# Moving the split of the projection weights from GpSimd to ScalarE and VectorE, a block of fills later in SyncE's queue, and the expert splits into another order

## The reference

```python
q = (layernorm(x) @ Wq)            # 16 heads of 64
k, v = (y @ Wkv)
res = softmax(q @ k.T * 64 ** -0.5) @ v
x = x + res @ Wproj + bproj
p = softmax(layernorm(x) @ gate_w); top 2 of 8, shares normalised
hidden = silu(h @ gate_w_e) * (h @ up_w_e)      # 512 wide
x = x + sum over the two of share * (hidden @ down_w_e)
```

## Time and profile before

| | |
|---|---|
| median of 3 runs | 1500.26 us (1498.55 to 1500.38) |
| the profiled execution | 1500.38 us |
| its span | 1498.6 us |
| PE busy | 1461.8 us (98%) |
| DVE, ACT, POOL busy | 950.6, 732.1, 550.7 us |
| mean granted TensorE clock | 0.994 |

### The profile page before, as it was taken

One profiled execution on the slowest core, in us unless ns is written; L12 is line 12 of the kernel. 1 busy time (PEld: TensorE's weight loads), 2 busy tenths in 40 slices (PEclk: granted clock), 3 DMA queues, 4 the chain that ended last, 5 costly groups with the idle time before them and its releaser, 6 DMA issues.

```text
span 1498.6 us, 37285 instructions
## 1 busy us (share of the span) xinstructions
PE 1461.8 (98%) x11882; PEld 1289.0 (86%) x11883; DVE 950.6 (63%) x2600; ACT 732.1 (49%) x2032; POOL 550.7 (37%) x641
## 2 busy tenths in 40 slices
PE   6999999999999999999999999999997999999997
PEld 5888889888888988898889888888886888888886
DVE  5667777677767776767777777767668543333332
ACT  4555555555555555555555555555556322222221
POOL 3424334343434343433334343434354332233222
PEclk9999999999999999999999999999998999999999
DMA  9222222222222222222222222213027233333332
GB/s 253 86 66 68 74 73 72 68 73 66 72 72 72 75 92 80 76 72 66 72 73 72 69 72 66 76 40 108 29 80 260 56 59 54 51 49 50 52 53 25
DMA packets 101105, 113.80 MB, mean 76 GB/s; under 512 B 17244, under 2 KB 88140, under 8 KB 101068
## 3 DMA queue, kind: packets, MB, share of 16 engines
q1 hardware_dynamic: 87900, 94.33, 20.6%
q0 software_dynamic: 12144, 15.66, 6.4%
q10 hardware_dynamic: 1024, 3.34, 0.7%
HBM read 61.37 MB, written 51.93 MB: 76 GB/s over the span
## 4 chain that ended last, share of the span: by engine, by line
PE 94%; DVE 3%; DMA 1%; issue 1%; ACT 0%; POOLq 0%; DVEq 0%; SPq 0%
PE bank L1375 25%; PE bank L1318 17%; PE bank L1444 11%; PE bank L1420 10%; PE bank L1410 9%; PE bank L1638 7%; PE bank L1465 6%; PE bank L1382 4%; PE bank L1622 2%; PE bank L1577 1%; DVE probT L1187 1%; DVE Wgu L1056 1%; PE bank L1492 1%; DMA WqL_whole<-in_L_xattn_Wq 1%; PE bank L1482 0%
## 5 line engine op out<-in xcount | busy, mean ns | idle before, releaser
L844 ACT ACTIVATE prob<-bank,neg_max 112x375 f32<-112x375 f32 x512 | 298.7, 588 | 135.7 <-DVE neg_max L1181 135.7
L1181 DVE TENSOR_REDUCE neg_max<-bank 112x1 f32<-112x375 f32 x512 | 243.7, 538 | 16.0 <-PE bank L1410 15.9
L1420 PE MATMUL bank<-ident,prob 112*125 112x112 f32 x1536 | 214.5, 273 | 2.7 <-ACT prob L844 2.4
L1420 PEld LDWEIGHTS bank<-ident,prob 112*125 112x125 f32 x1536 | 195.9, 188 | 13.8 <-ACT prob L844 4.8
L779 POOL DMA_INDIRECT out<-y_out,dest_now x63 | 98.1, 1557 | 221.6 <-ACT y_out L931 196.5
L1444 PE MATMUL bank<-probT,V 125*64 125x112 f32 x3072 | 176.5, 264 | 1.9 <-DVE probT L1187 1.1
L1318 PE MATMUL bank<-Wgu,hT_h 128*128 x504 | 177.1, 433 | 1.0 <-DVE hT_l L1247 1.0
L1444 PEld LDWEIGHTS bank<-probT,V 125*64 125x64 f32 x3072 | 149.0, 137 | 28.4 <-issue 25.1
L969 DVE TENSOR_TENSOR K_l<-bank,K_h 128x376 fp32r<-128x376 f32 x256 | 140.2, 549 | 51.6 <-ACT K_h L804 45.3
L959 DVE COPY V<-bank 125x512 f32<-125x512 f32 x96 | 66.4, 692 | 137.7 <-PE bank L1382 134.7
L802 ACT COPY V<-bank 125x512 f32<-125x512 f32 x96 | 56.3, 587 | 181.3 <-PE bank L1382 178.7
(11 more groups left out here) (196 smaller groups left out, 3587.8 us busy)
## 6 DMA issues: line engine op xcount, KB each, us to landing
bins<-pad_rows SPq DMA_DIRECT2D x29, 1032.0 KB, 5.8
inv_rows<-sums SPq DMA_DIRECT2D x126, 128.0 KB, 2.8
h_in<-bins SPq DMA_DIRECT2D x63, 129.0 KB, 2.1
Wgu<-in_L_ffn_gate_up_w SPq DMA_DIRECT2D x6, 1024.0 KB, 7.8
y_sb<-in_ctx SPq DMA_DIRECT2D x32, 187.5 KB, 2.6
y_sb<-in_ctx SPq DMA_DIRECT2D x62, 93.8 KB, 2.6
x_sb<-in_x SPq DMA_DIRECT2D x16, 224.0 KB, 2.9
x_res<-in_x SPq DMA_DIRECT2D x32, 112.0 KB, 2.4
```

Of the source, the lines that this page charges most:

```text
L844: nc.scalar.activation(prob[:, j, :], S_ps[j][0:LQ, 0:LKV], ACT.Exp, bias=neg_max[:, j:j + 1], accum_out=row_sum[:, head // HB, head % HB: ...
L1181: nc.vector.tensor_reduce(neg_max[:, j:j + 1], S_ps[j][0:LQ, 0:LKV], AX.X, ALU.max, negate=True).then_inc(max_done, 1)
L1420: last = nc.tensor.transpose(S_ps[j][0:KR, t * LQ:t * LQ + LQ], prob[:, j, t * KR:t * KR + KR], ident[0:LQ, 0:LQ])
```

## The change

Three things are changed.

1. SyncE: the wait for the split of b = 1 and the load of y of b = 3 stand ahead of the bins' fills instead of behind them.
2. The projection weights: GpSimd's `split_projection` (four copies and four subtractions on quarters, behind `split_O` of b = 0) is gone. ScalarE copies all of `WpH` in one instruction at the end of b = 0, s = 1, and VectorE subtracts all of `WpL` in one at the end of b = 0, s = 3.
3. The handover to the experts: ScalarE copies expert 4 before it issues the loads of experts 6 and 7, and expert 6 behind the rows of tiles 0 and 1 instead of ahead of them. VectorE subtracts experts 4 and 5 behind the rows instead of ahead of them.

```diff
             load_y(2, 0)
             sp.wait_ge(xn_done, 2)
             load_x(1)
+            sp.wait_ge(y_lo, 2)
+            sp.wait_ge(yB_lo, 2)
+            sp.wait_ge(yT_done, 2)
+            load_y(3, 1)
             sp.wait_ge(pads_ready, 1)
             sp.dma_start(bins[E * STRIDE:E * STRIDE + IDLE * P, :].rearrange("(n p) w -> p n w", p=P),
                          pad_rows[:].unsqueeze(1).to_broadcast([P, IDLE, W])).then_inc(idle_out, 16)
             for k in range(2):
                 prefill(k, k)
-            sp.wait_ge(y_lo, 2)
-            sp.wait_ge(yB_lo, 2)
-            sp.wait_ge(yT_done, 2)
-            load_y(3, 1)
...
-                    if known(b) and b == 0:
-                        split_projection()
...
                         for k in made_at["V"][:1]:
                             evacuate(a, k)
+                        if known(b) and b == 0 and s == 1:
+                            act.wait_ge(wp_in, 16)
+                            nc.scalar.copy(WpH[:].rearrange("p k n -> p (k n)"),
+                                           wp[:].rearrange("p k n -> p (k n)")).then_inc(wp_done, 1)
...
+            hi_of_experts(4, 5)
             act.wait_ge(pv_made, B * NS)
             for e in (6, 7):
                 load_expert(act, e)
...
             open_gates(B - 2, A_ps[1])
-            hi_of_experts(4, 7)
+            hi_of_experts(5, 6)
             for t in range(2):
                 hi_of_rows(t, t)
-            hi_of_experts(7, E)
+            hi_of_experts(6, E)
...
                         for k in made_at["V"][1:]:
                             low_part(a, k)
+                        if known(b) and b == 0 and s == 3:
+                            dve.wait_ge(wp_done, 1)
+                            nc.vector.tensor_tensor(WpL[:].rearrange("p k n -> p (k n)"), wp[:].rearrange("p k n -> p (k n)"),
+                                                    WpH[:].rearrange("p k n -> p (k n)").bitcast(F32),
+                                                    ALU.subtract).then_inc(wp_done, 1)
...
-            for e in (2, 3, 4, 5):
+            for e in (2, 3):
                 lo_of_expert(e)
             for t in range(2):
                 lo_of_rows(t, t)
                 keep_dest(t, 0, t)
-            for e in (6, 7):
+            for e in (4, 5, 6, 7):
                 lo_of_expert(e)
...
-                    pe.wait_ge(wp_done, 8)
+                    pe.wait_ge(wp_done, 2)
```

More of the change, by code:

```diff
@@ L684, in split_O @@
                 pool.tensor_tensor(lo, O_now[:], hi.bitcast(F32), ALU.subtract).then_inc(OT_lo, 1)
[L686 to L696, removed]
             def split_y(b, slot, free):
```

## The result

The changed kernel took 1510.12 us (median of 4 runs, 1509.52 to 1510.96) where the kernel before took 1499.60 us (4 runs). The ratio is 1.0070 with an interval of 1.0053 to 1.0089: about 10.5 us slower. The forecast of slower came true, the predicted 1505.9 us and the upper end of the range, 1509.8 us, were too low. The profiled execution took 1509.31 us, 8.9 us more than that of before, and its span is 8.9 us longer as well, 1507.5 us.

The account below looks back on a forecast made before the run. TensorE, busy 98% of the span, was taken as the bound, so its new waits cost: 0 + 0 + 1.06 + 1.6 + 2.85 = 5.5 us on 1500.38 gave 1505.9 us, range 1503.0 to 1509.8.

Parts of the forecast that it names:

- Part 1: SyncE's queue, first pair: inverses land at about 54.8 us, before O_now at 55.1; cost 0, bounds 0 and 2 us.
- Part 2, ScalarE: b = 0, s = 2: the weight copy delays exponentials, so TensorE's second transpose waits; cost 1.06 us, bounds 0.7 and 1.3.
- Part 2, VectorE: b = 1, s = 0: the 2.29 us subtraction delays maxima and exponentials, TensorE waits; cost 1.6 us, bounds 1.3 and 2.3.
- Part 2, GpSimd: Projection weights: taking four subtractions and four copies from GpSimd gives 0, since nobody waited for them.
- Part 3: Handover: four experts behind the rows delay `hid` and tile 0's down product; cost 2.85 us, bounds 2.2 and 2.9.
- The sum: Whole kernel: 0 + 0 + 1.06 + 1.6 + 2.85 = 5.5 us slower, giving 1505.9 us; chance 0.45.
- The clock falls: Rival: TensorE's new waits lower its clock, about 1.7 us each; 1507.6 us for one, 1509.3 for two; chance 0.28.
- the inverses come late: Rival, first pair: fills at 250 GB/s hold up the inverses and O_now, adding 2 us; 1507.9 us, chance 0.10.
- The copies are hidden: Rival, first pair: TensorE's stages have spare time, so only the handover costs; 1503.2 us, chance 0.09.
- not slower: Rival, handover: GpSimd's split of the last O runs freely, up to 3.5 us earlier; 1502.4 us, chance 0.04.

Follow-up runs that it names:

- part 1 alone: Kernel before with only SyncE's order changed (load of y of b = 3 ahead of the fills), against the kernel before: 1505.10 us, ratio 1.0029.

## Why the prediction was wrong

- **Part 1, where it failed.** "I take 0 for this part. Its bounds are 0 and 2 us." The mechanism stood there and was named, but the last step compared 54.8 us with 55.1 us and took the difference for cover. Measured in the changed kernel: the stored sums were through at 52.4 us and not at 51.3, and O_now started at 56.05 us with 1.53 us of waiting. By the marks the first O_now is 2.41 us late, of which ScalarE's copy alone makes 0.78; 1.6 us are the inverses. Counted from the first maximum, the loads of the inverses went out 0.9 us later than forecast (18.8 us instead of 17.9), and O_now started 3.56 us behind their issue where the forecast had 2.8; the two loads' issue alone takes 1.13 us. The fills went at 238 to 331 GB/s in the stretches of 36 to 50 us, and x_res, which lay behind three of them in the queue, had been held back at its issue for 2.5 us. An estimate that is good to a microsecond or two can't decide a race of 0.3 us. By the Trainium skill (DMA: Bandwidth & Descriptors, Queues, rings and completion order) each SDMA engine takes the descriptors of one ring in order; the trace is in keeping with it, a small store took 5.5 us behind a fill and 2.4 us without it.
- **The clock, the other half of the miss.** The prediction made a fall a rival with 0.28 and 1.7 us for each. It fell in two places where it had not before. In the first pair it fell in all three profiles that have O_now waiting for the rows (the change twice, part 1 alone), and in none of the others; it cost 1.5 us between first and second O_now. At the handover it fell behind the wait for `hid` of 2.8 to 4.0 us in all five profiles with four experts behind the rows, and cost 1.4 to 2.7 us by the last `y_out` (1.5 in the changed kernel by the end of the span). Both stood behind waits that the change made, in eight cases of eight, so they belonged to terms of the sum and were not a chance of their own. Part 2's waits for exponentials in the first pair, 0.75 us at most, had no fall behind them.
- **Part 2, ScalarE.** 1.06 us predicted, 0.78 measured. The first exponential was 1.11 us late instead of 1.27 (the copy began 0.1 us before the V block's copy was through), and 0.34 us of it, not 0.21, was taken up by the second.
- **Part 2, VectorE.** 1.6 us predicted, 1.88 us in the profile.
- **Part 2, GpSimd.** Nothing gained, as predicted: its relief ended in a longer idle time of VectorE.
- **Part 3.** 2.85 us predicted, 2.75 measured to the first down product. The gate product came 0.5 us earlier after the last O_now (11.07 us instead of 11.57), predicted 0.6. The single profile's 2.75 is closer than the scatter between profiles allows to claim; the means of the two groups differ by 2.7. TensorE waited 3.9 us for `hid`, not nearly 3, because its products ran at the full rate. ScalarE's order and the loads cost nothing, as predicted.
- **The sum.** 1.6 + 0.78 + 1.88 + 1.5 in the first pair and 2.75 + 1.5 at the handover are 10.0 us. The profile's 8.9 is that less the 0.4 us of an earlier start and the 0.8 us of the stretch between, and the timed 10.5 is near it. The forecast 5.5 lacked the inverses (1.6) and the two falls (3.0). With only one of the two missing, 7.1 or 8.5 us, the time would have stayed inside the range.
- **The rivals.** *The clock falls* and *the inverses come late* both came true at once. *The copies are hidden* and *not slower* did not. OT_l took 3.05 us again, behind experts 2 and 3.

What stays open: why VectorE's subtraction alone loses 3.4 us in time and 1.9 in its profile (the interval reaches down to 1.9), how much one expert behind the rows costs, whether the parts save something on each other, and what decides that the clock falls behind one wait and not behind another of the same length (below).

## What to carry to other kernels

A bulk transfer that nobody waits for still has a place in a queue: before it is moved, look for the next small transfer behind it that somebody does wait for, and if the two estimates come out within a microsecond, price it as lost. Where the change makes TensorE wait for some 1.6 us or more in a stretch that was full, as here, price the wait with a fall of the clock first, and let the wait without one be the rival; shorter waits had none in part 2. And work that goes to an idle engine gains nothing if it lands on one that feeds the critical engine in the same stage.

## What the runs showed of the hardware

- The waits at `O_now` of 1.6, 2.2 and 2.9 us for TensorE were followed by a fall of its clock to 0.50 for 3.4 us every time, and the waits for `hid` of 2.8 to 4.0 us by one of 6.8 us. The length of a wait alone doesn't decide it. All profiles have two waits of 0.9 to 1.0 us for exponentials between 1117 and 1133 us, and three of them, that of before among them, a fall behind these (0.55 and 0.60 of clock from 1128 to 1132 us). Waits for `probT` of 1.45 to 1.7 us near 1140 us had no fall until the wait for `OT_l` in seven profiles, and one 6 us later in an eighth.
- One DMA's issue took 0.58 us in its usual place and 2.50 us behind three fills of about 1 MB that were still under way.
- VectorE's low part of y took 0.55 us without and 1.38 us with a GpSimd subtraction beside it.
